# Attention and output weights loaded in place of their low parts; squares and key bias issued earlier

## The reference, cut to what matters

```
h = xf @ W_proj + b_proj                        # 1024 x 1024
y = layernorm(h) * g + b
w = softmax(y @ W_wgen + b_wgen)                # 8 heads x 5 taps
out = h + relu(conv(y, w) @ W_ff + b_ff)        # causal 5-tap conv, then 1024 x 1024

q, k, v = split(layernorm(h) @ w_qkv.T + b_qkv) # 3 x 512 columns, 8 heads of 64
h = h + (softmax(causal(k, q)) v) @ w_o.T + b_o # per sequence of 64 tokens

h = h + unperm(gelu(perm(layernorm(h)) @ up) @ down)   # 16 heads, 64 -> 256 -> 64
```

## Time and profile before

| | us |
|---|---|
| Median of three executions | 1031.88 |
| The profiled execution | 1035.96 |
| its span, first to last instruction | 1034.2 |
| TensorE busy | 967.4 |
| VectorE busy | 509.2 |
| ScalarE busy | 424.4 |
| GpSimd busy | 394.3 |

### The profile page before, as it was taken

How to read it: one execution, slowest core, us unless ns; L and a number is a source line. 1 busy time by engine, 2 the same in 40 slices (tenths; PEclk the granted TensorE clock), 3 DMA queues, 4 the chain that set the end, 5 groups by cost and what they waited for, 6 DMA issues and landing times.

```text
span 1034.2 us, 15644 instructions
## 1 busy us (share of the span) xinstructions
PE 967.4 (94%) x6108; PEld 714.5 (69%) x6108; DVE 509.2 (49%) x848; ACT 424.4 (41%) x753; POOL 394.3 (38%) x317
## 2 busy tenths in 40 slices
PE   7999999987899999999879999999999999889996
PEld 5777777776777788778657877877887777323331
DVE  6153535659447502254756256256064567755551
ACT  6144444555433533434243243243132332356553
POOL 1225252227601122723361451451023377748532
PEclk9999999999899999999989999999999999899998
DMA  8542725395343154327100201200214975533421
GB/s 290 209 165 4 205 7 181 4 285 203 117 145 107 62 126 164 109 95 265 41 11 22 92 11 35 79 11 22 92 52 149 289 260 209 184 111 133 149 77 61
DMA packets 75062, 124.96 MB, mean 121 GB/s; under 512 B 29159, under 2 KB 38375, under 8 KB 70894
## 3 DMA queue, kind: packets, MB, share of 16 engines
q1 hardware_dynamic: 68830, 107.03, 33.7%
q0 software_dynamic: 5120, 16.78, 4.6%
q10 hardware_dynamic: 1040, 0.16, 0.1%
HBM read 81.46 MB, written 42.50 MB: 120 GB/s over the span
## 4 chain that ended last, share of the span: by engine, by line
PE 53%; issue 10%; POOL 7%; DVE 5%; DMA 3%; ACT 2%; another core or an unknown queue 1%; POOLq 0%; SPq 0%; DVEq 0%; ACTq 0%
PE bank L299 14%; PE bank L301 13%; PE bank L300 13%; PE bank L1795 3%; PE bank L1804 3%; POOL vacc L335 2%; PE bank L1551 1%; POOL out L758 1%; POOL acc L363 1%; DVE sq L377 1%; DMA stage<-w_qkv_t 1%; POOL acc L308 1%; DVE acc L1219 1%; PE bank L1523 1%; DMA db_late<-h_s 1%
## 5 line engine op out<-in xcount | busy, mean ns | idle before, releaser
L335 POOL TENSOR_TENSOR vacc<-vacc,sq 128x512 f32<-128x512 f32 x72 | 97.2, 1350 | 45.8 <-ACT sq L381 36.4
L299 PE MATMUL bank<-xa_h,wp_h 128*128 128x512 f32 x256 | 103.4, 404 | 7.2 <-DVE xa_l L1094 7.2
L299 PE MATMUL bank<-cv_h,wf_h 128*128 128x512 f32 x256 | 106.3, 415 | 1.2 <-POOL wf_l L293 1.2
L301 PE MATMUL bank<-cv_h,wf_l 128*128 128x512 f32 x256 | 101.4, 396 | 0.0
L300 PE MATMUL bank<-cv_l,wf_h 128*128 128x512 f32 x256 | 101.4, 396 | 0.0
L300 PE MATMUL bank<-xa_l,wp_h 128*128 128x512 f32 x256 | 101.1, 395 | 0.0
L301 PE MATMUL bank<-xa_h,wp_l 128*128 128x512 f32 x256 | 101.1, 395 | 0.0
L700 POOL TENSOR_TENSOR fo<-fo,res 128x512 f32<-128x512 f32 x32 | 43.5, 1373 | 123.4 <-ACT fo L837 89.8
L1077 ACT ACTIVATE gt<-bank 128x512 f32<-128x512 f32 x128 | 66.2, 600 | 39.0 <-PE bank L1795 36.8
L1795 PE MATMUL bank<-dd,up_f 64*128 64x512 f32 x256 | 67.9, 651 | 5.6 <-ACT gt L1077 5.4
L381 ACT ACTIVATE sq<-sq 128x512 f32<-128x512 f32 x56 | 35.1, 632 | 79.3 <-DVE sq L377 79.3
(11 more groups left out here) (179 smaller groups left out, 2167.5 us busy)
## 6 DMA issues: line engine op xcount, KB each, us to landing
xs<-x_t SPq DMA_DIRECT2D x32, 256.0 KB, 6.2
h_s<-ho SPq DMA_DIRECT2D x8, 1024.0 KB, 5.9
res<-h_s SPq DMA_DIRECT2D x32, 256.0 KB, 3.6
h_s<-fo SPq DMA_DIRECT2D x32, 256.0 KB, 2.4
dc<-h_s SPq DMA_DIRECT2D x4, 2048.0 KB, 9.3
h<-h_s SPq DMA_DIRECT2D x8, 1024.0 KB, 10.5
h_s<-h SPq DMA_DIRECT2D x8, 1024.0 KB, 4.8
stage<-w_qkv_t SPq DMA_DIRECT2D x24, 256.0 KB, 3.6
```

What stands on the lines that cost most here:

```text
L299: pe.matmul(o, wh, xh, start=start, stop=False)
L301: return pe.matmul(o, wl, xh, start=False, stop=stop)
L335: g.tensor_tensor(vacc[:, :], t[:, 0, :] if k == 1 else vacc[:, :], t[:, k % 2, :], ALU.add).then_inc(ln_pool, 1)
```

## The change

The value, query, key and output weights are no longer loaded into `stage`. Each has a raw view (`wv_r`, `wq_r`, `wk_r`, `wo_r`) at the bytes of its own low part, and the low part is made in place. High and low parts of the value and query weights change places in R2. The loads of these units (`raw_load`) wait until TensorE has used the `w_ff` or `cv_l` blocks that lie there (a new counter `ff_used`, raised with each block k of the last group of the last chunk), or, for `w_o`, until the values of the last chunk are done. Nine semaphores (`RAW = 9`) mark the landings, so a load also waits for the low part nine units before it. SP issues all eight value loads before the store of block 4, two units before the store of block 6, two before that of block 7, and the other twelve after it, with `c_load(1)` behind them all. ScalarE makes four value high parts ahead of the last two relus, and all query and key high parts ahead of the value copies. TensorE starts the values when the first four relus of the last chunk are done. In chunk 0 ScalarE makes the squares of the next chunk ahead of the query bias of pair 1, and VectorE makes six of eight `xc_low` before the key bias of pair 3 and two after it.

```
+        wk_r = place("wk_r", [P, KB, PART], F32, R1 + 48 * KIB)
+        wv_l = place("wv_l", [P, KB, PART], F32R, R2)
+        wv_r = place("wv_r", [P, KB, PART], F32, R2)
+        wv_h = place("wv_h", [P, KB, PART], F32R, R2 + 16 * KIB)
+        wq_l = place("wq_l", [P, KB, PART], F32R, R2 + 32 * KIB)
+        wq_r = place("wq_r", [P, KB, PART], F32, R2 + 32 * KIB)
+        wq_h = place("wq_h", [P, KB, PART], F32R, R2 + 48 * KIB)
+        wo_r = place("wo_r", [P, PAIRS, D], F32, R2 + 16 * KIB)
...
+                units.append((... wv_h[:, k, :], wv_l[:, k, :], "v", wv_r[:, k, :], k // 2 + 1))
...
+                for col, h, l, who, r, dead in ((0, wq_h, wq_l, "g" if k < 4 else "v", wq_r, k // 2 + 1),
+                                                (1, wk_h, wk_l, "v", wk_r, k + 1)):
...
+        def raw_load(e, u):
+            src, _, _, _, raw, dead = units[u]
+            if dead is None:
+                e.wait_ge(v_mm, 4 * CH)
+            elif dead == KB:
+                e.wait_ge(ff_mm, 8 * CH)
+            else:
+                e.wait_ge(ff_used, dead)
+            if u - RAW >= U_V:
+                who = 0 if units[u - RAW][3] == "v" else 1
+                e.wait_ge((w_lo_v, w_lo_g)[who], lo_before[who][u - RAW + 1])
+            e.dma_start(raw, src).then_inc(w_ld[(u - U_V) % RAW], 16)
...
-                if c == CH - 1:
-                    for u in range(U_V, U_V + 4):
-                        unit_load(sp, u)
                 for m in range(KB):
+                    if c == CH - 1:
+                        for u in {4: range(U_V, U_QK), 6: range(U_QK, U_QK + 2), 7: range(U_QK + 2, U_QK + 4)}.get(m, ()):
+                            raw_load(sp, u)
                     ff_store(c, m)
...
-            for u in range(U_V + 4, U_QK + 8):
-                unit_load(sp, u)
+            for u in range(U_QK + 4, U_O):
+                raw_load(sp, u)
             c_load(1)
-            for u in range(U_QK + 8, U_O):
-                unit_load(sp, u)
...
                 for m in range(3, 6):
                     ff_relu(c, m)
+                if not ahead:
+                    for k in range(4):
+                        act.wait_ge(ff_used, 4 + k // 2 + 1)
+                        unit_hi(act, U_V + k)
...
-            for u in range(U_V, U_V + 16):
+            for u in range(U_V + 4, U_O):
                 unit_hi(act, u)
...
             c_values(0, range(TILES))
-            for u in range(U_V + 16, U_O):
-                unit_hi(act, u)
             c_qk(0, 0)
...
                 c_softmax_exp(c, 0)
+                if ahead and not later:
+                    c_squares(c + 1)
...
                 c_pt(c, 0)
-                if ahead and not later:
-                    c_squares(c + 1)
...
                 if ahead:
-                    for k in range(KB):
+                    for k in range(LOW_FIRST):
                         xc_low(c + 1, k)
                 c_qk(c, 3)
+                if ahead:
+                    for k in range(LOW_FIRST, KB):
+                        xc_low(c + 1, k)
...
+                if g == 2 and c == CH - 1 and k < KB - 1:
+                    mm.then_inc(ff_used, 1)
...
-                if isinstance(c, int) and c == 0:
-                    pe.wait_ge(ff_ev, 8 * CH)
+                if c == 0:
+                    pe.wait_ge(ff_ev, 8 * (CH - 1) + TILES)
...
+                if m == 0 and first:
+                    pe.wait_ge(ff_ev, 8 * CH)
...
+RAW = 9
+LOW_FIRST = 6
```

More of the change, by code:

```diff
@@ L161, in audio_tower @@
         masks_ok = sem("masks_ok")
-        stage_ld = [sem(f"stage_ld{i}") for i in range(4)]
+        w_ld = [sem(f"w_ld{i}") for i in range(RAW)]
+        ff_used = sem("ff_used")
         w_hi = sem("w_hi")
@@ L237, in weight_units @@
             for k in range(KB):
-                units.append((w_qkv_t[k * P:(k + 1) * P, 2 * PART:3 * PART], wv_h[:, k, :], wv_l[:, k, :], "v"))
+                units.append((w_qkv_t[k * P:(k + 1) * P, 2 * PART:3 * PART], wv_h[:, k, :], wv_l[:, k, :], "v",
+                              wv_r[:, k, :], k // 2 + 1))
             for k in range(KB):
-                for col, h, l, who in ((0, wq_h, wq_l, "g" if k < 4 else "v"), (1, wk_h, wk_l, "v")):
+                for col, h, l, who, r, dead in ((0, wq_h, wq_l, "g" if k < 4 else "v", wq_r, k // 2 + 1),
+                                                (1, wk_h, wk_l, "v", wk_r, k + 1)):
                     units.append((w_qkv_t[k * P:(k + 1) * P, col * PART:(col + 1) * PART],
-                                  h[:, k, :], l[:, k, :], who))
+                                  h[:, k, :], l[:, k, :], who, r[:, k, :], dead))
             for half in range(2):
@@ L245, in weight_units @@
                     cols = slice(half * N, half * N + N)
-                    units.append((w_o_t[k * P:(k + 1) * P, cols], wo_h[:, k, cols], wo_l[:, k, cols], "g"))
+                    units.append((w_o_t[k * P:(k + 1) * P, cols], wo_h[:, k, cols], wo_l[:, k, cols], "g",
+                                  wo_r[:, k, cols], None))
             return units
@@ L266, in wait_units, with unit_landed @@
                 e.wait_ge(w_lo_g, lo_before[1][upto])
+        def raw_load(e, u):
[10 more added lines that the diff above has]
+            e.dma_start(raw, src).then_inc(w_ld[(u - U_V) % RAW], 16)
+        def unit_landed(e, u):
+            if u >= U_V:
+                i = (u - U_V) % RAW
+                e.wait_ge(w_ld[i], 16 * ((u - U_V) // RAW + 1 + (U_V // 4 if i < 4 else 0)))
+            else:
+                e.wait_ge(w_ld[u % 4], slot_count(u))
         def unit_load(e, u):
@@ L273, in unit_load @@
             src = units[u][0]
-            e.dma_start(stage[:, u % 4, :], src).then_inc(stage_ld[u % 4], 16)
+            e.dma_start(stage[:, u % 4, :], src).then_inc(w_ld[u % 4], 16)
         def slot_count(u):
@@ L280, in unit_views @@
         def unit_views(u):
-            return stage[:, u % 4, :], units[u][1], units[u][2]
+            raw = units[u][4] if u >= U_V else stage[:, u % 4, :]
+            return raw, units[u][1], units[u][2]
         def unit_hi(act, u):
-            act.wait_ge(stage_ld[u % 4], slot_count(u))
+            unit_landed(act, u)
             st, h, _ = unit_views(u)
@@ L290, in unit_lo @@
             e.wait_ge(w_hi, u + 1)
-            e.wait_ge(stage_ld[u % 4], slot_count(u))
+            unit_landed(e, u)
             st, h, l = unit_views(u)
```

## The result

The changed kernel took 1017.70 us (median of four executions, 1016.52 to 1018.22), the kernel before 1032.04 in the same comparison. The ratio is 0.9871, with a 95% interval of 0.9849 to 0.9894. That is 14.3 us less; 12.5 had been forecast, with 1019.4 us as the time. In a second comparison the two stood at 1021.44 and 1033.70 (ratio 0.9858, 0.9828 to 0.9887). One of the 23 executions of the kernel before that stand beside the first four experiments took 1376 us at a granted clock of 0.654; it is left out of their ratios.

What follows compares the result with a forecast made beforehand. TensorE was taken to bound the kernel: its work plus time standing still or at lower clock. Savings of 2.4 + 4.7 + 2.8 + 2.6 = 12.5 us from the 1031.9 median gave 1019.4 us, range 1014 to 1026.

Steps and rivals of the forecast that it cites:

- Part 1, start of the values: Between phase B's last matmul and the first value matmul: TensorE's lost 2.38 us go; ends 1.4 and 2.38.
- Part 2, pauses of pair 0: First 48 query and key matmuls: pauses from late weights go, gaining 4.7 us, all or nothing.
- Part 3, old stall with its low clock: First variance of chunk 1: 7.2 us go, 5.17 of waiting and 2.0 of lower clock.
- Part 3, new wait at the scores of pair 1: Counted from T, start of pair 0's scores (504.67): TensorE waits 2.84 us for the query bias behind the squares.
- Part 3, low clock behind it: Behind the new wait at pair 1's scores: lower clock costs 1.6 us, between ends 0 and 2.0.
- Part 4, key bias, three chunks: Scores of pair 3 in chunks 0, 1 and 2: each 0.89 us sooner, 2.6 us in all; ends 0 and 2.7.
- Part 5, output weights: Loads wait for the last chunk's values: nothing gained or lost; without cover at most 8.6 us.
- The slack of part 2: Query and key weights of pair 0: 15 us of slack for the weights, 5 for the value copies.
- the addition may slip by a microsecond: End of phase B: residual 6 lands at 463.9 behind the eight value loads; TensorE loses nothing.
- The rival on the value copies: ScalarE's copies wait behind all high parts, idling TensorE: 1037 us at 18 us beyond about 484; chance 0.03.
- stalls of the profiled run: Some pauses belong to the profiled execution, so 4.1 us cannot be saved twice: 1023.5 us; chance 0.12.
- The rival that the change doesn't do what it says: SP blocks on `ff_used`, loads gain no lead, parts 1 and 2 give nothing: 1026.5 us; chance 0.06.

Runs made afterwards that it cites:

- the first four experiments: Kernel before with only new loads and early values, only squares, or only key bias changed; changed kernel without early value high parts: 1023.52, 1026.83, 1029.58, 1021.21 us.
- late_queries: Changed kernel with the first four query and key units issued behind phase B's last store: 1022.61 us against 1035.24 for the kernel before, ratio 0.9899.
- keybias_only: Kernel before with two of the eight low parts behind the key bias of pair 3, nothing else: 1029.58 us against 1030.98, ratio 0.9988.
- late_start: Changed kernel with the first four value high parts made behind the last two relus again: 1021.21 us, ratio 0.9916 to the kernel before.
- slots4: Changed kernel with four landing semaphores in place of nine (RAW = 4): 1028.21 us against 1033.70 for the kernel before, ratio 0.9941.
- copies_mid: Changed kernel with ScalarE's value copies back between the first and last eight query and key high parts: 1022.79 us against 1035.24 for the kernel before, ratio 0.9889.
- squares_only: Kernel before with the squares of chunk 1 ahead of the query bias of pair 1, nothing else: 1026.83 us against 1030.98, ratio 0.9973.

## Why the prediction was right

Point by point, with the size forecast and the size measured in the ledger, first profile against first:

| Step | Forecast | Measured |
|---|---|---|
| Part 1, start of the values | 2.38 | 2.38 |
| Part 2, pauses of pair 0 | 4.7 | 4.74 |
| Part 3, old stall with its low clock | 7.2 | 7.2 (gone) |
| Part 3, new wait at the scores of pair 1 | 2.84 | 2.61 (16.18 - 13.57) |
| Part 3, low clock behind it | 1.6 | 1.55 (15.19 against the 13.64 of `late_queries`, which had none) |
| Part 4, key bias, three chunks | 2.6 | 2.7 (0.86 and 1.86) |
| Part 5, output weights | 0 | 0 seen |
| Sum | 12.5 | 12.9 |

- The step that carried most was to count the squares' chain from T and to see that it ends past the query bias. The bracket in the profile after reads 3.10 us, but an idle time also holds the 0.45 us that stood there before. What is new is some 2.6 us, a little less than the 2.84 forecast.
- The clock was the only term taken between far ends (0 and 2.0). Taken by the nearest stall of the earlier trace rows it fitted the profile, and both profiles of the changed kernel. In part that is luck: the same wait went without low clock in two of seven profiles, where the term is nothing. And the prediction's other row for the clock does not hold as a rule. It read from the earlier trace rows that 2.22 us of idle time bring no low clock; in `keybias_only` and `late_start` they did, at a cost of 1.6 to 1.7 us. So part 1 could have gained some 4 us where 2.38 was taken.
- **The slack of part 2 was mis-sized.** I had the last high part at 479 and 5 us of room ahead of the value copies. It ended at 483.27, with 0.4 us of room. The step that failed is the one on the residual: "the addition may slip by a microsecond". It slipped by 1.9 us (465.90 against 463.99), the store behind it to 467.67, and the two query and key units behind it and all later ones with it. The residual itself had been issued at 459.82, as forecast, behind the eight value loads, and GpSimd waited for it until 465.90, where 463.9 had been forecast. In all eight profiles with this order of loads the addition starts 5.1 to 6.1 us behind that issue, where I had taken 4.1 for the landing; that the value loads ahead of it on SP's queue are the cause was not tested. The first generation of the query and key loads then took longer than I gave it: unit 46 was issued at about 470.8 instead of 468, its low part began at 476.80 and ended at 478.34, 7.5 us after the issue instead of 6, and the last load went out at 478.41 instead of 474. The sum did not suffer, but by luck: 0.4 us of room was left. `late_queries` shows it: there the copies start 1.5 us later behind the first value matmul, and TensorE stands still for 0.66 us.
- The rival on the value copies was real: `slots4` shows its place and about its rate. The copies started 7.8 us later behind the first value matmul, of which 0.4 was room, and it cost 7.2 us there.
- The rival "stalls of the profiled run" was half right. The profile of before did hold 4.3 us that its second profile lacks, and 1.6 us more further on; the 4.1 us that I had worked out from the medians may be the same time, but executions without a profile cannot show it. But these lie in the last phase and not at the edited places, so nothing of the gain was lost to them. They made the profiles differ by 19.4 us where the medians differ by 14.3.
- The rival that the change doesn't do what it says fell at the start of the values: SP was through with the value loads at 459.3, where I had 459.

## What to carry to other kernels

Before an in-order engine is given a chain of work earlier, ask what short instruction now stands behind it and who waits for that: here some 2.6 us of new wait, and 1.6 us of low clock in five of seven profiles, were bought with the squares, and cutting the chain in two, six and two, gave both back. Room for transfers in flight can come from memory that the result itself will fill, if the raw value lies where its own remainder goes. And compare two profiles by distances between fixed places, not by their ends: single executions of this kernel differ by more than two of its four edits are worth.

## What the runs showed of the hardware

- A wait of TensorE of 3.1 us was followed by about seven steps of 0.43 us, 1.2 GHz, in both profiles of the changed kernel. Waits of 2.8 to 3.1 us at this place were followed by such steps in five of seven profiles, the wait of 2.22 us at the start of the values in two of five, and the wait of 2.44 to 2.52 us of the earlier trace rows in all thirteen. Two waits of equal length at the same instruction went both ways (3.08 us in `late_start` and in `copies_mid`), so the length of the wait alone does not decide.
- In the last phase too the same instructions at the same distances were followed once by a lower clock and once not. Add 13 to add 14 took 7.9 us, at a granted clock of 0.78, in the first profile of before and in those of `squares_only` and `keybias_only`, and 6.24 to 6.26, at 1.00, in all others, the second profile of before among them. TensorE's idle time there was 0.44 or 0.45 us each time. What decides it stays open.
- The low part of a unit takes VectorE 0.69 us alone and 1.78 beside a GpSimd addition. GPSIMD Engine Reference, section Specifications, of the Trainium skill says that GpSimd shares its interfaces to on-chip memory with VectorE, and that VectorE instructions with two inputs there contend for them. The low part is such an instruction, and the two durations agree with it. In `copies_mid`, where five such low parts fell beside the sum, the query and key block took 2.4 us more.
